# A graph attention, mixture-of-experts and graph convolution kernel: smaller expert groups with resident second weights, part rows gathered earlier, and a count's column table in PSUM

## The chip, the cores and the metric

One core of a Trainium2 chip runs the whole program. The metric is device microseconds (us) of one execution, as the median of the runs shown; the profile is of one further execution. The engines are TensorE (PE; its weight loads are listed apart as PEld), VectorE (DVE), ScalarE (ACT), GpSimd (POOL) and SyncE (SP, which only issues DMAs).

## What is computed

Four layers on 6250 nodes of 256 features and 200000 edges, each added to the residual `x` after a layer norm. Only the first two are touched by the change, and the third uses a table that the second prepares.

```python
# layer 1: graph attention, 8 heads of 32
e = leaky_relu(a_src[src] + a_dst[dst], 0.2)
e_exp = exp(e - segment_max(e, dst)[dst])
alpha = e_exp / (segment_sum(e_exp, dst)[dst] + 1e-16)
x = x + relu(segment_sum(h[src] * alpha[:, :, None], dst) + bias)
# layer 2: 8 experts, the best 2 for each node, 256 -> 512 -> 256
y = sum over e of (gelu(xn @ W1[e] + b1[e]) @ W2[e] + b2[e]) * w_full[..., e]
# layer 3: graph convolution with in and out degrees; layer 4: 8 experts with a capacity
```

## The kernel before

**The attention loop** (`gat_edges`, L1102) goes over 104 steps of 16 edge tiles. For each step POOL issues 16 gathers of 128 rows (L1262) into a ring of four buffers, and each engine works through a fixed order of parts of neighbouring steps, its `slot`. On DVE (L1432) a slot begins with `count_onehots` (L1337): two comparisons (L1344) of a column table `iob`, `count_iota` in SBUF in bfloat16, with the halves of the sources' numbers; TensorE later sums the one-hots to the degrees (L1525). After them come `totals` (L1349), which wait for the terms that TensorE turns (L1493) once the step's last gather has landed and ACT has packed its terms (L1274), then the sums into the residual (L1430) and the `messages` (L1407), which read the numerators that ACT wrote to PSUM (`numerators`, L1277). The end of a ring buffer's use, `sc`, lets POOL gather again (L1259).

**Rows and logits** (`rows_and_logits`, L1642, with `AttentionRows`, L1569) make the layer-1 result, its norm and the router's logits; SP meanwhile writes zeros over 12.8 MB of the expert output (`zero_fill`, L1772). **Routing** (`route`, L2430) is a chain on DVE that ends with 98 pairs of one-hot comparisons (L2593, L2594), each followed by a product on TensorE (L2631). POOL has nothing to do in it.

**The first experts** (`experts`, L2635) take the sorted slots in 56 groups of 256 (`TOK1`), each of one expert, in 14336 slots in all. For a group POOL gathers two tiles of rows (L2693), TensorE turns them (L2725), DVE scales them into `xT` (L2777), TensorE makes the hidden product from `w1s`, whose columns it takes with a stride of four (`f:F:FC`, L2735), ACT applies the activation (L2761), TensorE makes the output from `hT` and `w2s` (L2745), DVE adds `b2` (L2788), and POOL scatters two tiles (L2700). SP loads `w1`, `b1`, `w2` and `b2` of the group's expert for each group into one of two buffers (L2675 to L2679). A float32 product is two weight loads and two matmuls in the trace, a turn only one of each.

Beside the experts runs `DenseTables` (L708), which prepares the 62 code tables of layer 3: POOL gathers part rows (L755), DVE subtracts (L767), TensorE turns them in float32 (L782), ACT copies (L796), SP stores (L740). As there are only 56 groups, the last six run together in tick 1 (`rest`). `staged` (L142) orders the stages on every engine: two ticks written out for each of the first two rounds, then a loop of two ticks a round. On TensorE a tick is: hidden of the group before, turn of the codes, turn of this group, output of the group before.

The lines that order TensorE's tick and set the hidden product:

```python
staged(pe, groups, [(1, hidden), (1, side.turn(pe)), (0, turn), (1, outs)], 2)          # L2752
pe.matmul(ph[:, f % 2, 0:tok], w1s[:, b, c, f:F:FC], xT[:, b, c, :], start=c == 0, stop=c == 1)  # L2735
```

Of the kernel before, what the change touches and what calls it, by code (L numbers as in the profile page):

```python
# [19 lines left out]
P = 128  # L20
# [7 lines left out]
TOK1 = 256  # L28
# [91 lines left out]
class RoundTable:  # L120

    def __init__(self, nc, engine, row, depth, lag, top):
        self.nc, self.engine, self.row, self.depth, self.lag, self.top = nc, engine, row, depth, lag, top
        self.at = {}

    def fetch(self, i):
        start = i * self.depth - self.lag
        skip = -start if isinstance(start, int) and start < 0 else 0
        n = self.depth - skip
        _, values = self.nc.values_load_multi_w_load_instructions(
            self.row[:, bass.ds(start + skip, n)], engines=(self.engine,), min_val=0, max_val=self.top,
            skip_runtime_bounds_check_because="the table's rows were clamped to their range when they were built")
        for j in range(n):
            self.at[(skip + j - self.lag) % self.depth] = values[j]


def staged(eng, steps, stages, depth, tables=()):  # L142
# [15 lines left out]
    def fetch(i):  # L158
        for table in tables:
            table.fetch(i)  # L160

    rounds = steps // depth
    for i in range(2):
        fetch(i)
        for j in range(depth):
            tick(i, j)
    with eng.Fori(2, rounds) as i:
        fetch(i)
        for j in range(depth):
            tick(i, j)  # L170
    if any(lag for lag, _ in stages):
        fetch(rounds)
    for j in range(max(lag for lag, _ in stages)):
        tick(rounds, j)
# [532 lines left out]

class DenseTables:  # L708


    def __init__(self, k, S, C, T, ctx):
        self.nc, self.S, self.C, self.T = k.nc, S, C, T
        self.rest = S.SUPER - S.G1
        assert S.G1 % 2 == 0 and self.rest > 0
        self.rg = k.sems("part_rows_gathered", 2)
        self.xg = k.sem("rest_rows_gathered")
        self.xs = k.sem("rest_codes_stored")
# [4 lines left out]
        self.vr = k.sb(ctx, "part_rows", [P, 2, 2, P])  # L722
        self.vx = k.sb(ctx, "rest_rows", [P, self.rest, 2, P])
        self.row = k.sb(ctx, "codes_out", [P, 2, 2 * P], BF16)
        self.rx = k.sb(ctx, "rest_codes_out", [P, self.rest, 2 * P], BF16)
        self.pt = k.ps(ctx, "codes_ps", [P, 512])

    def order(self, t):

        return t if isinstance(t, int) and t < 2 else t + self.rest  # L730

    def rest_at(self, t):

        return range(self.rest) if isinstance(t, int) and t == 1 else ()

    def store(self, sp):
        def put(n, s, row, sem):
            sp.wait_ge(self.tc, n + 1)
            sp.nop(nofuse=True)
            sp.dma_start(self.T.codes[bass.ds(s, 1), :, :].rearrange("a p c -> p (a c)"), row).then_inc(sem, 16)  # L740

        def stage(i, b, t, first):
            put(self.order(t), t, self.row[:, b, :], self.cs[b])
            for x in self.rest_at(t):
                put(2 + x, self.S.G1 + x, self.rx[:, x, :], self.xs)
        return stage

    def stored(self, sp):
        for m in range(2):
            sp.wait_ge(self.cs[m], 16 * (self.S.G1 // 2))  # L750
        sp.wait_ge(self.xs, 16 * self.rest)

    def gather(self, pool, t):
        def take(s, out, sem):
            pool.indirect_dma_start(  # L755
                out=out.rearrange("p a e -> p (a e)"), out_offset=None, in_=self.T.gnn[:, :],
                in_offset=bass.IndirectOffsetOnAxis(ap=self.C.vpart[:, s:s + 1], axis=0)).then_inc(sem, 16)
        if t >= 2:
            pool.wait_ge(self.tp, self.order(t - 2) + 1)
        take(t, self.vr[:, t % 2, :, :], self.rg[t % 2])  # L760
        for x in self.rest_at(t):
            take(self.S.G1 + x, self.vx[:, x, :, :], self.xg)

    def compare(self, dve):
        def stage(i, b, t, first):
            dve.wait_ge(self.rg[b], i * 16 + 16)
            dve.tensor_scalar(self.vr[:, b, 0, :], self.vr[:, b, 0, :], self.C.vcode[:, bass.ds(t, 1)], None,  # L767
                              ALU.subtract).then_inc(self.cr, 1)
            for x in self.rest_at(t):
                s = self.S.G1 + x  # L770
                dve.wait_ge(self.xg, 16 * self.rest)
                dve.tensor_scalar(self.vx[:, x, 0, :], self.vx[:, x, 0, :], self.C.vcode[:, s:s + 1], None,
                                  ALU.subtract).then_inc(self.cr, 1)
        return stage

    def turn(self, pe):
        def turned(n, rows):
            pe.wait_ge(self.cr, n + 1)
            if not isinstance(n, int) or n >= 1:
                pe.wait_ge(self.tc, n)  # L780
            for a in range(2):
                last = pe.transpose(self.pt[:, a * P:(a + 1) * P], rows[:, a, :], self.C.ident[:, :])  # L782
            last.then_inc(self.tp, 1)

        def stage(i, b, t, first):
            turned(self.order(t), self.vr[:, b, :, :])
            for x in self.rest_at(t):
# [2142 lines left out]
```

## Time and profile before

| | us |
|---|---|
| three runs, median (lowest, highest) | 5123.05 (5122.59, 5126.46) |
| the profiled execution | 5124.75 |
| its span, first to last instruction | 5122.9 |
| PE, DVE, POOL, ACT busy in the span | 4174.7, 3459.0, 2300.1, 1648.5 |
| mean granted TensorE clock | 0.841 |

The span falls into stages that follow each other, with all engines meeting at the end of each. A busy share over the whole span says little, as the limit changes from stage to stage; a stage is read from its own stretch. The granted clock is a share of 2.4 GHz; it has two levels, 1.0 and 0.5, and a mean between them is a mixture.

### The profile page before, as it was taken

The page shows a single profiled execution, that of the slowest core. Times are in us where ns is not written, and L with a number is a line of the kernel's source. Part 1 is how long each engine was busy: PE and PEld are TensorE (multiplying, and loading weights), DVE is VectorE, ACT ScalarE, POOL GpSimd, SP SyncE. Part 2 cuts the span into 40 slices and gives each one's busy share as a digit, 9 for nine tenths or more (in the row PEclk, how much of TensorE's full clock was granted, in tenths as well). Part 3 has the DMA queues.
Part 4 walks back from the last instruction along what each step waited for, and adds up shares of the span by engine and source line. Part 5 has one row for each costly group of instructions (what it writes and reads, how often), then busy time and mean ns, then how long its engine had stood idle before and what let it go on. Part 6 is the DMA issues. An engine that isn't in the chain of part 4 may idle for free. (4 is left out here: it accounts for less than half of the span.)

```text
span 5122.9 us, 87171 instructions
## 1 busy us (share of the span) xinstructions
PE 4174.7 (81%) x27202; PEld 3066.2 (60%) x27203; DVE 3459.0 (68%) x7696; ACT 1648.5 (32%) x2854; POOL 2300.1 (45%) x2330
## 2 busy tenths in 40 slices
PE   3477777777777777776699964799999999958998
PEld 2355555555555555555489953466666666557787
DVE  6366766676667667768622237899998999764444
ACT  1233333333333333333122236333333333231211
POOL 1377777777777777774155620000000000024553
PEclk9677777777777777776799986899999999958999
DMA  4766666666666666656167653454545545453432
GB/s 122 188 164 164 168 162 164 163 169 162 163 165 168 162 163 165 167 157 207 63 218 232 233 176 111 87 98 85 97 87 90 93 89 95 85 184 115 136 122 87
DMA packets 978900, 733.38 MB, mean 143 GB/s; under 512 B 735781, under 2 KB 864352, under 8 KB 976628
## 3 DMA queue, kind: packets, MB, share of 16 engines
q1 hardware_dynamic: 863047, 427.75, 32.6%
q0 software_dynamic: 109264, 296.24, 21.0%
q10 hardware_dynamic: 6364, 6.40, 0.4%
q8 instruction: 141, 2.31, 0.2%
q14 instruction: 84, 0.68, 0.0%
HBM read 485.07 MB, written 92.30 MB: 113 GB/s over the span
## 5 line engine op out<-in xcount | busy, mean ns | idle before, releaser
L1262 POOL DMA_INDIRECT gat_rows<-h_rows,gat_sources x1664 | 1621.9, 975 | 509.9 <-issue 478.8
L1520 PE MATMUL gat_sum_ps<-gat_rows,gat_onehot 128*128 128x265 f32 x3328 | 1261.7, 542 | 3.7 <-DVE gat_rows L1407 3.6
L1520 PEld LDWEIGHTS gat_sum_ps<-gat_rows,gat_onehot 128*128 128x128 f32 x3328 | 861.3, 272 | 218.2 <-DVE gat_rows L1407 4.8
L2207 ACT CAST gnn_z<-build_ps 128x392 bf16<-128x392 f32 x992 | 479.7, 485 | 749.4 <-PE build_ps L2222 749.2
L2231 PE MATMUL back_ps<-zb_pieces,gnn_z 128*128 128x384 bf16 x3038 | 634.6, 325 | 0.0
L2253 PE MATMUL front_ps<-x_res_wide,front_rows 128*128 128x448 bf16 x2604 | 618.1, 351 | 0.0
L2148 DVE TENSOR_TENSOR onehot_low<-dense_codes,dense_iota_bf 128x2048 bf16<-128x2048 bf16 x496 | 603.9, 1218 | 2.0 <-PE build_ps L2222 1.9
L2127 POOL DMA_INDIRECT front_rows<-zf_piece_rows,vrow_nodes x62 | 58.8, 948 | 1148.0 <-PE front_ps L2253 1137.9
L1407 DVE TENSOR_TENSOR gat_rows<-gat_rows,gat_numerators_ps 128x1024 f32<-128x1024 f32 x416 | 502.2, 1207 | 0.0
L2222 PEld LDWEIGHTS build_ps<-onehot_high,onehot_low 128*128 128x128 bf16 x7936 | 352.6, 98 | 184.9 <-issue 38.2
L2735 PE MATMUL moe_hidden_ps<-moe_rows_T,moe_w 128*128 128x256 f32 (+1 forms) x1408 | 450.4, 475 | 2.3 <-DMA moe_b<-in_L_ffn_b 1.5
L2761 ACT ACTIVATE moe_hidden<-moe_hidden_ps,moe_b 128x256 f32<-128x256 f32 (+1 forms) x352 | 194.0, 551 | 765.3 <-PE moe_hidden_ps L2735 765.3
L2745 PE MATMUL moe_out_ps<-moe_w,moe_hidden 128*128 128x256 f32 x1920 | 434.8, 384 | 1.1 <-ACT moe_hidden L2761 1.1
L2735 PEld LDWEIGHTS moe_hidden_ps<-moe_rows_T,moe_w 128*128 128x128 f32 x1408 | 377.5, 322 | 65.3 <-issue 4.8
L2222 PE MATMUL build_ps<-onehot_high,onehot_low 128*128 128x49 bf16 x7936 | 373.5, 188 | 44.0 <-DVE onehot_high L2148 41.5
L1430 DVE TENSOR_TENSOR x_res_wide<-x_res_wide,gat_sum_ps 128x265 f32 x832 | 355.7, 428 | 66.9 <-DVE x_res_wide L1430 66.4
L2745 PEld LDWEIGHTS moe_out_ps<-moe_w,moe_hidden 128*128 128x128 f32 x1920 | 360.1, 190 | 63.0 <-issue 13.9
L2231 PEld LDWEIGHTS back_ps<-zb_pieces,gnn_z 128*128 128x128 bf16 x3038 | 263.2, 97 | 150.7 <-issue 1.3
L1280 ACT ACTIVATE gat_numerators_ps<-gat_exponents 128x128 f32<-128x128 f32 x104 | 29.3, 281 | 906.2 <-DVE gat_exponents L1400 759.4
L2160 DVE TENSOR_TENSOR gnn_z<-gnn_z,front_ps 128x448 f32<-128x448 f32 x434 | 267.8, 617 | 74.8 <-PE front_ps L2253 73.3
L1493 PE MATMUL gat_turned_ps<-ident,gat_src_terms 128*128 128x128 f32 x104 | 49.3, 474 | 324.7 <-ACT gat_src_terms L1274 324.7
L2253 PEld LDWEIGHTS front_ps<-x_res_wide,front_rows 128*128 128x128 bf16 x2604 | 222.9, 97 | 139.8 <-issue 0.3
(377 smaller groups left out, 5467.5 us busy)
## 6 DMA issues: line engine op xcount, KB each, us to landing
moe_w<-in_L_ffn_W SPq DMA_DIRECT2D x112, 512.0 KB
gat_targets<-gat_step_targets SPq DMA_DIRECT2D x104, 512.0 KB
moe_w<-in_L_ffn_w SPq DMA_DIRECT2D x32, 1024.0 KB
gat_rows<-h_rows,gat_sources POOLq DMA_INDIRECT x1664
gat_flags<-gat_tile_flags SPq DMA_DIRECT2D x104, 128.0 KB
normal_rows<-moe_xn_all SPq DMA_DIRECT2D x14, 896.0 KB
mid_taken<-moe_rows_out SPq DMA_DIRECT2D x14, 896.0 KB, 7.4
moe_rows_out<-slot_zeros SPq DMA_DIRECT2D x24, 512.0 KB
```

The source lines that it names most:

```text
L1262: pool.indirect_dma_start(out=g[:, b, t, :], out_offset=None, in_=T.h[:, :], in_offset=bass.IndirectOffsetOnAxis(ap=idx[:, b, t:t + 1], ax ...
L1407: dve.tensor_tensor(rows[:, :, :, 0:HD], rows[:, :, :, 0:HD], pW[:, n * PART:(n + 1) * PART, :].unsqueeze(3).to_broadcast([P, PART, H, HD] ...
L1430: dve.tensor_tensor(window(w), window(w), po[:, s % BANKS, 0:W], ALU.add).then_inc(ad, 1)
L1520: last = pe.matmul(po[:, s % BANKS, 0:W], o[:, b, s * SUB + t, :], g[:, b, s * SUB + t, :], start=t == 0, stop=t == SUB - 1)
L2148: last = dve.tensor_tensor(out[:, n, :, :, :], ct[:, k % SLOTS, a, at].rearrange("p (u t) -> p u t", t=HITS).unsqueeze(2) .to_broadcast(sh ...
L2160: dve.tensor_tensor(yfT[:, at:at + CN], yfT[:, at:at + CN], pf[:, n, 0:CN], ALU.add).then_inc(ya, 1)
L2207: nc.scalar.copy(AT[:, k % 2, :, CHUNK * c:CHUNK * (c + 1)], pb[:, c % 2, 0:CHUNK * NT].rearrange("p (u h) -> p h u", u=CHUNK)).then_inc(a ...
L2222: last = pe.matmul(pb[:, c % 2, u * NT:(u + 1) * NT], ol[:, n, i, :, t], oj[:, n, i, :, t], start=True, stop=True)
L2231: ins = pe.matmul(py[:, (k - 1) % 2, 0:3 * P], AT[:, (k - 1) % 2, h, :], zb3[:, h, :, :].rearrange("p s f -> p (s f)"), start=h == 0, stop ...
L2253: ins = pe.matmul(pf[:, bank, 0:CN], zfv[:, first + s, m * P:(m + 1) * P], AV[:, first + s, chunk * CN:(chunk + 1) * CN], start=n == 0, st ...
L2735: last = pe.matmul(ph[:, f % 2, 0:tok], w1s[:, b, c, f:F:FC], xT[:, b, c, :], start=c == 0, stop=c == 1)
L2745: last = pe.matmul(py[:, q % 2, 0:D], hT[:, f, q * P:(q + 1) * P], w2s[:, b, f, :], start=f == 0, stop=f == FC - 1)
```

## The change

- `TOK1` is 128: the first experts run in 106 groups of 128 slots (13568 slots), in a function of their own, `resident_experts`. The second weights of all eight experts (`w2`, 4 MB) and `b1` are loaded once by SP during rows and logits; `b2` of all experts once at the start of the experts. Per group SP loads only `w1`. The hidden product takes contiguous columns of `w1`. The output product and the biases take the expert by a register; each of PE, ACT and DVE loads four group numbers a round for that (`Choice.fetch`).
- The output of a group comes two ticks after its turn (one before), with two buffers for `hT` and a PSUM bank for each of the four hidden slices.
- All 62 gathers of part rows go to POOL in routing (`gather_parts`); the code tables are turned in bfloat16, in the first 62 ticks.
- Only the pad rows of the expert output are zeroed (2 DMAs of 22 rows instead of 25 DMAs).
- In the attention loop the column table of the count is a float32 table in PSUM, in the bank of the numerators; `count_onehots` waits for the numerators of its step first.

```diff
-TOK1 = 256
+TOK1 = 128
 class DenseTables:
+    def start(self, dve):
+        dve.tensor_copy(self.ident[:, :], self.C.ident[:, :]).then_inc(self.ir, 1)
+        dve.wait_ge(self.pg, 16 * self.S.SUPER)
     def compare(self, dve):
         def stage(i, b, t, first):
-            dve.wait_ge(self.rg[b], i * 16 + 16)
-            dve.tensor_scalar(self.vr[:, b, 0, :], self.vr[:, b, 0, :], self.C.vcode[:, bass.ds(t, 1)], None,
+            if not first:
+                dve.wait_ge(self.tp, t - 1)
+            rows = self.parts[:, bass.ds(t, 1), :, :].rearrange("p s a e -> p (s a) e")
+            dve.tensor_copy(self.code[:, b, 1, :], rows[:, 1, :])
+            dve.tensor_scalar(self.code[:, b, 0, :], rows[:, 0, :], self.C.vcode[:, bass.ds(t, 1)], None,
                               ALU.subtract).then_inc(self.cr, 1)
...
 gat_edges:
-        iob = k.sb(ctx, "count_iota", [P, P, 2], BF16)
-        pW = k.ps(ctx, "gat_numerators_ps", [P, TILES, H])
+        pWI = k.ps(ctx, "gat_numerators_ps", [P, 512])
+        pW = pWI[:, 0:TH].rearrange("p (t h) -> p t h", h=H)
+        iob = pWI[:, TH:TH + 2 * P].rearrange("p (w t) -> p w t", t=2)
             def count_onehots(j, i, a):
                 dve.wait_ge(cl[b], i * 16 + 16)
+                dve.wait_ge(ex, j + 1)
...
 AttentionRows.load:
-        self.filled = zero_fill(sp, [self.y1[0:2 * self.S.ROWS, :], *self.more], self.zf, self.zs)
+        pads = self.S.ROWS - self.S.N
+        for a in range(2):
+            sp.dma_start(self.y1[a * self.S.ROWS + self.S.N:(a + 1) * self.S.ROWS, :], self.zf[0:pads, :]).then_inc(self.zs, 16)
+        self.weights.load(sp)
...
 route:
+        if tables is not None:
+            @block.gpsimd
+            def _(pool):
+                gather_parts(pool, S, C, tables, k.parts, k.pg)
...
+def resident_experts(k, S, C, T, tag, groups, func, W, xn, y, src_of, dst_of, gtab, affine):
+        @block.sync
+            sp.dma_start(b2[:, :, :].rearrange("p e d -> p (e d)"), W.dram[3].rearrange("e d -> (e d)").partition_broadcast(P)).then_inc(bl, 16)
+            def load(i, b, t, first):
+                e = sp.value_load(gtab[0:1, bass.ds(t, 1)], min_val=0, max_val=W.X - 1)
+                if not first:
+                    sp.wait_ge(hp, (t - 1) * FC)
+                    sp.nop(nofuse=True)
+                sp.dma_start(w1s[:, b, :, :], W.dram[0][bass.ds(e, 1), :, :].rearrange("a (c p) f -> p (a c) f", p=P)).then_inc(wl[b], 16)
+            phased(sp, groups, [(0, None, load), (2, S.SUPER, side.store(sp))], 2)
+        @block.gpsimd
+            for t in range(groups + 4):
+                if t < groups:
+                    take(t)
+                if t >= 4:
+                    put(t - 4)
+        @block.tensor
+            def hidden(i, b, t, first):
+                pe.wait_ge(tc, t + 1)
+                pe.wait_ge(wl[b], i * 16 + 16)
+                for f in range(FC):
+                    if not (first and b == 0):
+                        pe.wait_ge(hc, t * FC + (f + 1 - FC))
+                    for c in range(2):
+                        last = pe.matmul(ph[:, f, 0:P], w1s[:, b, c, f * P:(f + 1) * P], xT[:, b, c, :],
+                                         start=c == 0, stop=c == 1)
+                    last.then_inc(hp, 1)
+            def outs(i, b, t, first):
+                e = expert.at(2, b)
+                pe.wait_ge(hc, t * FC + FC)
+                for f in range(FC):
+                    last = pe.matmul(py[:, b, 0:D], hT[:, b, f, :], W.w2[:, bass.ds(e, 1), f, :].rearrange("p a d -> p (a d)"),
+                                     start=f == 0, stop=f == FC - 1)
+            pe.wait_ge(side.ir, 1)
+            pe.wait_ge(W.wl, W.full)
+            phased(pe, groups, [(1, None, hidden), (1, S.SUPER, side.turn(pe)), (0, None, turn), (2, None, outs)], 2, expert.fetch)
+        @block.scalar
+            phased(act, groups, [(0, None, hidden), (0, S.SUPER, side.copy(act))], 2, expert.fetch)
+        @block.vector
+            dve.wait_ge(bl, 16)
+            side.start(dve)
+            phased(dve, groups, [(0, None, turned), (2, None, outs), (0, S.SUPER, side.compare(dve))], 2, expert.fetch)
```

`phased` is `staged` with a tick count at which a stage ends (62 for the code tables) and a call at the start of each round, in which the registers are loaded.

## Rows read from the trace of the kernel before

**Rows 1.** Busy by stretch: stretch, length, PE, PEld, DVE, ACT, POOL, clock, DMA, GB/s.
```profile
194.00:2324.00 2130.00, 1626.01 (x7892) 1170.55 (x7892) 1473.71 (x3799) 701.96 (x724) 1621.94 (x1664) 0.75 0.62 164
...
2454.00:2532.00 78.00, 46.55 (x200) 31.47 (x200) 70.73 (x275) 1.53 (x2) 0.00 (x0) 0.76 0.00 1
2543.00:3013.00 470.00, 465.46 (x2136) 422.00 (x2136) 120.00 (x284) 123.68 (x286) 270.55 (x279) 0.99 0.68 224
```

**Rows 2.** Groups, attention loop: count, busy us, mean ns, idle before by releaser.
```profile
L1262 POOL DMA_INDIRECT gat_rows<-h_rows,gat_sources x1664 | 1621.9, 975 | 509.9 <-issue 478.8 <-PE gat_sum_ps L1520 27.7 <-DMA gat_sources<-step_sources 3.4
...
L1407 DVE TENSOR_TENSOR gat_rows<-gat_rows,gat_numerators_ps 128x1024 f32<-128x1024 f32 x415 | 501.0, 1207 | 0.0
L1430 DVE TENSOR_TENSOR x_res_wide<-x_res_wide,gat_sum_ps 128x265 f32 x824 | 352.3, 428 | 65.8 <-DVE x_res_wide L1430 65.6 <-PE gat_sum_ps L1520 0.2
...
L1344 DVE TENSOR_TENSOR count_onehot_lo<-count_halves,count_iota 128x2048 bf16<-128x2048 bf16 x104 | 127.4, 1225 | 63.9 <-PE gat_sum_ps L1520 62.2 <-issue 1.8
...
L1344 DVE TENSOR_TENSOR count_onehot_hi<-count_halves,count_iota 128x784 bf16<-128x784 bf16 x104 | 58.2, 559 | 0.0
```

**Rows 3.** Timeline of one attention step: start us, length us, engine, line, idle before.
```profile
1202.17 1.22 DVE L1407 TENSOR_TENSOR gat_rows<-gat_rows,gat_numerators_ps 128x1024 f32<-128x1024 f32 x1
1202.55 0.94 POOL L1262 DMA_INDIRECT gat_rows<-h_rows,gat_sources  x1 [0.30 <-issue]
...
1214.53 0.21 ACT L1283 ACTIVATE gat_factors<-gat_exponents 1x8 f32<-1x8 f32 x1
...
1215.12 0.95 POOL L1262 DMA_INDIRECT gat_rows<-h_rows,gat_sources  x1 [0.30 <-issue]
1215.58 1.23 DVE L1344 TENSOR_TENSOR count_onehot_lo<-count_halves,count_iota 128x2048 bf16<-128x2048 bf16 x1 [0.51 <-PE gat_sum_ps L1520]
...
1216.37 1.25 POOL L1262 DMA_INDIRECT gat_rows<-h_rows,gat_sources  x1 [0.30 <-issue]
...
1220.51 0.42 DVE L1353 TENSOR_TENSOR_SCAN gat_running<-gat_flags,gat_turned_ps 128x128 f32<-128x128 f32 x1 [3.23 <-PE gat_turned_ps L1493]
```

**Rows 4.** Timeline of TensorE in one tick of the first experts.
```profile
2701.11 4.07 PE L2735 MATMUL moe_hidden_ps<-moe_rows_T,moe_w 128*128 128x256 f32 x16
2705.01 0.38 PE L782 MATMUL codes_ps<-ident,part_rows 128*128 128x128 f32 x2
2705.23 0.60 PE L2725 MATMUL moe_turn_ps<-ident,moe_rows 128*128 128x128 f32 x4
2705.81 3.71 PE L2745 MATMUL moe_out_ps<-moe_w,moe_hidden 128*128 128x256 f32 x16
2709.37 0.93 PE L2735 MATMUL moe_hidden_ps<-moe_rows_T,moe_w 128*128 128x256 f32 x3
```

**Rows 5.** Timeline of the weight loads in a stretch of the attention loop.
```profile
1206.61 0.52 PEld L1504 LDWEIGHTS gat_small_ps<-gat_tile_carries,gat_head_select_T 8*128 8x128 f32 x4 [0.35 <-issue]
1207.05 0.08 PEld L1506 LDWEIGHTS gat_small_ps<-ident,gat_previous 8*1 8x1 f32 x1
```

**Rows 6.** Timeline at the start of the first experts.
```profile
2542.94 5.76 PE L2735 MATMUL moe_hidden_ps<-moe_rows_T,moe_w 128*128 128x256 f32 x16 [1.02 <-DMA moe_b<-in_L_ffn_b]
...
2569.25 2.97 PE L2735 MATMUL moe_hidden_ps<-moe_rows_T,moe_w 128*128 128x256 f32 x12
```

**Rows 7.** Timeline at the end of the first experts.
```profile
3009.07 3.72 PE L2745 MATMUL moe_out_ps<-moe_w,moe_hidden 128*128 128x256 f32 x16 [0.34 <-ACT moe_hidden L2761]
```

**Rows 8.** DMA issues by line, whole span: KB each, median us from issue to landing.
```profile
unit_codes<-codes_out SPq DMA_DIRECT2D x56, 64.0 KB, 4.8
```

**Rows 9.** Timeline around the start of routing: last logits copy, first operation.
```profile
2453.68 0.17 ACT L1738 COPY moe_raw_logits<-moe_po 128x8 f32<-128x8 f32 x1 [1.06 <-PE moe_po L1768]
...
2454.16 0.57 DVE L2498 TENSOR_TENSOR moe_logits<-moe_raw_logits,b_router 128x392 f32<-128x392 f32 x1 [17.00 <-PEq L1658]
```

**Rows 10.** Timeline at routing's end.
```profile
2531.43 0.22 DVE L2606 TENSOR_SCALAR moe_slot_source<-moe_slot_token 128x112 int32<-128x112 f32 x1
```

**Rows 11.** Timeline of SP's DMA issues in rows and logits.
```profile
2370.65 25.17 SPq L1779 DMA_DIRECT2D moe_rows_out<-slot_zeros  x25
```

More of the change, by code:

```diff
@@ L117, in join, with staged @@
         self.eng.wait_ge(self.sem, self.n)
[L120 to L142, printed above, removed]
+def staged(eng, steps, stages, depth):
     def tick(i, j):
@@ L749, in stored @@
         for m in range(2):
[L750 to L762, printed above, removed]
+            sp.wait_ge(self.cs[m], 16 * (self.S.SUPER // 2))
@@ L781, in turned @@
             for a in range(2):
-                last = pe.transpose(self.pt[:, a * P:(a + 1) * P], rows[:, a, :], self.C.ident[:, :])
+                last = pe.transpose(self.pt[:, a * P:(a + 1) * P], self.code[:, b, a, :], self.ident[:, :])
             last.then_inc(self.tp, 1)
-        def stage(i, b, t, first):
-            turned(self.order(t), self.vr[:, b, :, :])
-            for x in self.rest_at(t):
-                turned(2 + x, self.vx[:, x, :, :])
         return stage
@@ L2661, in experts @@
         py = k.ps(ctx, f"{tag}_out_ps", [P, 2, 512])
-        side = DenseTables(k, S, C, tables, ctx) if tables is not None else None
         if final is not None:
@@ L2705, in _ @@
                     take(t)
-                if side is not None and 1 <= t <= groups:
-                    side.gather(pool, t - 1)
                 if t >= 2 and final is None:
@@ L2747, in outs @@
                     last.then_inc(yp, 1)
[L2749 to L2752 removed]
+            staged(pe, groups, [(1, hidden), (0, turn), (1, outs)], 2)
         @block.scalar
@@ new lines, with __init__, fetch, at @@
+class Choice:
+    def __init__(self, nc, engine, table, top):
+        self.nc, self.engine, self.table, self.top = nc, engine, table, top
+    def fetch(self, i):
+        first = max(2 * i - 2, 0) if isinstance(i, int) else i * 2 - 2
+        n = min(2 * i + 2, self.table.shape[1]) - first if isinstance(i, int) else 4
+        _, self.values = self.nc.values_load_multi_w_load_instructions(
+            self.table[0:1, bass.ds(first, n)], engines=(self.engine,), min_val=0, max_val=self.top,
+            skip_runtime_bounds_check_because="the groups' experts were clamped to their range when they were written")
+        self.shift = 2 - (2 * i - first) if isinstance(i, int) else 0
+    def at(self, lag, slot):
+        back = -(-(lag - slot) // 2) if lag > slot else 0
+        return self.values[2 - 2 * back + slot - self.shift]
```

244 lines of the change are left out of this document (170 added, 74 removed).

## The prediction

> **What bounds the kernel now.** I read the clock and busy time by stretch first, because the limit changes from stage to stage, and then three stages that the change touches [rows 1]. In the attention loop (2130 us) no engine is near full by its busy share: PE 1626, POOL 1622, DVE 1474. The groups by line give the answer: POOL's 1664 gathers are busy 1621.9 us and idle 509.9 us before themselves, and of that 478.8 is "issue", its own 0.30 us between two gathers [rows 2]. Busy and issue fill the stretch, so POOL bounds this loop, at 0.95 + 0.30 = 1.25 us a gather, 16 gathers a step. One step's timeline shows what makes it longer: the gather at 1216.37 takes 1.25 where its neighbour takes 0.95, and it is the one that starts while DVE compares for the count (L1344); DVE itself then waits 3.23 us for the terms TensorE turns, which wait for the gathers' landing [rows 3]. In the first experts (470 us) PE is busy 465 at a granted clock of 0.99, DVE 120, ACT 124, POOL 271: TensorE bounds it [rows 1]. Routing (78 us) is DVE's, busy 71, with POOL idle [rows 1].
>
> **The attention loop.** Mean gather 975 ns, unhindered 0.95 us: 1664 x 0.025 = 41 us of lengthening [rows 2, 3]. Both comparisons read two tables in SBUF; the sums (L1430) and messages (L1407) read one in SBUF and one in PSUM, run all through the loop, and the gather beside a message keeps 0.94 [rows 3]. With its table in PSUM the count becomes of that second kind, so I take the whole 41 us off. The price is on DVE: L1430 and L1407 take 428 ns for 265 columns and 1207 for 1024, that is 156 ns and 1.03 ns a column, so 2048 and 784 columns take 2.26 and 0.96 us in place of 1.23 and 0.56 [rows 2]: 1.43 us more a step. It lies before `totals`, where DVE waits 3.23 us; with a step 0.4 us shorter about 1.4 us of that wait is left, so it is covered. If the cover were gone, each uncovered 0.1 us a step would cost 10 us. The new wait for the numerators holds up the whole DVE slot, but ACT's last numerator write starts at 1214.53 and ends 0.8 us before the count begins [rows 3]: nothing. Only in the last slots, with no gather behind them, one longer count shows: 1.4 us. Sum: **-40 us**. Bounds: 0 if the lengthening has another cause, -57 with every gather at 0.94.
>
> **The first experts.** A tick of 256 slots runs from hidden to hidden 8.26 us: hidden 16 records from 2701.11 to 2705.01, 0.244 each; two code turns 0.22; four turns to the output's start 0.58; output 16 records to 2709.37, 0.2225 each [rows 4]. In the new tick of 128 slots the output has 8 records of the same form, 1.78. The hidden product has 16 records of 128 columns and not 256. Its nearest rows are the turns: pairs of a contiguous 128-column weight load and a 128-column matmul start every 0.11 us (2705.01 to 2705.23) [rows 4]. That this also holds for weights of an ordinary float32 product is seen in the attention loop, where four such loads follow each other in 0.44 us, 0.11 each [rows 5]. The 0.244 today against 0.2225 for the output is the strided load, which goes. So 16 x 0.11 = 1.76, and two turns 0.22. The codes' turns in bfloat16 have no row; between nothing and 0.22 for two I take 0.11, in 62 of 106 ticks. The 0.14 us that now lies between turns and output is a wait for the activation; an output that lags two ticks has its input long before. I leave 0.05 a tick for register loads. A tick: 1.76 + 0.22 + 1.78 + 0.06 + 0.05 = 3.87 us, 106 of them 410 us. The last output adds 2, the first ticks at the lower clock 4 (the first hidden product takes 5.76 for 4.07 [rows 4, 6]): 416 us. Today the same stretch is from 2542.94 to 3009.07 + 3.72, 470 us [rows 6, 7]; that includes some 10 us for the six `rest` codes and the slow first ticks, as 2569.25 is the third hidden product and two ticks take 16.5. Sum: **-54 us**.
>
> What must stay hidden: one `w1` load. Today w1, b1, w2 and b2 (1.16 MB) leave just before the code store on one queue, and that store, last of them, lands 4.8 us after its issue, with no wait for weights on PE; at the stretch's 224 GB/s 512 KB take 2.3 us [rows 1, 8], so one `w1` lands between 2.3 and 4.8 us after its issue, an estimate. It is issued when the hidden product two groups back ends and needed two ticks after that one began: 7.7 - 1.8 = 5.9 us. POOL issues 212 gathers and scatters at 0.97 + 0.30, 270 us of 410; DVE and ACT stay under half. Bounds of the tick: 3.72 with no gaps; 5.7 if a 128-column record cost as much as a 256-column one, which the 0.11 speaks against.
>
> **Routing and what moves.** POOL gets 62 gathers at 1.25 us, 77.5 us. Routing runs from 2454.16 to 2531.65, 77.5 us [rows 9, 10] and a little longer with 106 groups in its tables. The two chains are even, so each lengthened gather counts. In routing's first 30 us most DVE operations read two SBUF tables; 24 gathers fall there, and at 0.30 a hit, with all or none hit, that is 0 to 7 us. I take the queue of POOL to end 5 us after DVE's old end: **+5 us**. The zeros (25 DMAs, 25.17 us of SP's issuing [rows 11]) give way to 2 pad and 9 weight DMAs; the stage ends with ACT's logits copy at 2453.68 [rows 9], so nothing. `b2` (1 MB) now precedes the first `w1` on SP and holds back DVE, and with it the first turn; today 1.16 MB lies before the first hidden product: nothing, bounds -2 and +4.
>
> **Sum.** 5124.75 - 40 - 54 + 5 = 5036 for the profiled execution, which is 1.7 us over the median; so 5034 us. About 0.2% (10 us) is what a measurement of this kernel can tell from no change.
>
> **Rivals.**
> *The gathers stay long.* What lengthens them is DVE's load on SBUF as such, or the next operation takes the count's place under a gather. For it: only one place of a step shows it. Against: L1430 and L1407 write as much. Time: 5034 + 41 = 5075. Chance 0.10.
>
> *Weight loads set the pace of the hidden product.* With 128 columns a load is no longer shorter than its matmul, and a little that does not overlap shows in each of 1696 records. At 0.16 a record, about the middle between the 0.11 of 128 columns and the 0.2225 of 256, the tick is 0.80 longer: 106 x 0.80 = 85, 5119 us. Against: pairs at 0.11 [rows 4, 5], though those are few in a row. The Trainium skill, "TensorE: Matmul & The Clock Gate", section "Back-to-back issue gap", says a stream of load and matmul pairs at 128 columns sustains about 81 ns where an isolated gap would be 56; by that ratio the 0.11 would be the 0.16 of this rival. The trace disagrees as far as its short runs go. Chance 0.08, half of it faster and half the same.
>
> *Slower: TensorE's clock falls.* Twice as many hand-overs (turn, copy by DVE, hidden product) in each 256 slots; if one is late in each tick, by the weights or the turned rows, PE is no longer full. The attention loop, with PE busy 1626 of 2130, is granted a mean of 0.75, the experts 0.99 [rows 1]. At the lower level a tick doubles to 7.6 us and the stage to some 810 us: 5430. It decides from a tick of 4.7 us: 106 x 4.7 + 6 = 504, which eats 470 plus the 35 gained elsewhere. Against: two copies of 128 columns take DVE 0.6 us by the same 156 ns and 1.03 ns a column, and the 1.78 us of output lie between. Chance 0.07, with DVE's longer count overrunning its 1.4 us of cover on the same side.
>
> *Routing holds on longer*, POOL 15 us behind: 5044, chance 0.08, inside the range.
>
> **How the numbers follow.** The forecast has 0.67, with 5013 (tick without gaps, routing even) to 5060 (tick 4.1). The range 5010 to 5080 adds the first and last rivals, 0.85 together. Faster: 0.67 + 0.10 + 0.08 + 0.04 = 0.89; same 0.04; slower 0.07.
>
> **What would show it.** In the profile after: L1262's mean at 0.95 and the loop near 2090 us; L1344 at 2.3 and 1.0 us; DVE's wait before L1353 near 1.4; hidden records every 0.11 us and hidden to hidden 3.9 us at a clock of 1.0; POOL's gathers filling routing. I am wrong if L1262 still shows 1.25 us gathers once a step, if PE waits for weights or turned rows in the experts, or if their clock is under 0.95.

## The result and the profile after

The changed kernel takes **5030.49 us** (median of four runs, 5029.82 to 5031.65) where the kernel before takes 5124.76 beside it (5122.59 to 5126.56): a ratio of 0.9817, 95% interval 0.9805 to 0.9829. The forecast was 5034 us, faster. The profiled execution has a span of 5028.0 us, 94.9 less than the 5122.9 before.

Where the 94.9 us come from is read off the two timelines at the same landmarks. Up to the first gather 2.1 us are lost, which is spread: in the traces of the runs below with the same code there, the first gather starts between 194.0 and 198.3 us. From the first gather to the out-degrees, the attention loop with its tail, it is 2161.8 against 2119.9 us: -41.9, of which the gathers give -44.6 and the tail behind the last gather, with one longer count in the way, takes back 2.7 (33.4 to 36.1; 33.3 again in the run below with the table back in SBUF). From there to the first operation of routing: nothing (97.3 both times). From that to the first hidden product 88.8 against 92.6: +3.8. From the first hidden product to the end of the last output 469.9 against 410.5: -59.3. The rest of the program: +0.4.

Busy time by stretch comes first (stretch, length, PE, PEld, DVE, ACT, POOL, clock, DMA, GB/s): attention loop, routing with the wait behind it, first experts, as in [rows 1].

```profile
197.00:2281.00 2084.00, 1573.86 (x7892) 1116.37 (x7892) 1623.56 (x3798) 701.88 (x724) 1577.22 (x1664) 0.78 0.63 168
2414.30:2500.50 86.20, 45.85 (x200) 32.17 (x200) 72.51 (x275) 1.53 (x2) 61.27 (x62) 0.74 0.30 95
2507.00:2925.00 418.00, 408.78 (x2878) 380.65 (x2878) 142.02 (x440) 173.21 (x487) 203.65 (x210) 0.99 0.64 207
```

POOL lost 45 us of busy time in the first line and DVE gained 150, POOL now works in the second, and the third is shorter at the same clock of 0.99. The groups of the attention loop answer to [rows 2] (count, busy us, mean ns, idle before by releaser):

```profile
L1244 POOL DMA_INDIRECT gat_rows<-h_rows,gat_sources x1664 | 1577.2, 948 | 510.0 <-issue 486.5 <-PE gat_sum_ps L1503 20.1 <-DMA gat_sources<-step_sources 3.4
...
L1327 DVE TENSOR_TENSOR count_onehot_lo<-count_halves,gat_numerators_ps 128x2048 bf16<-128x2048 bf16 x103 | 235.6, 2288 | 68.0 <-PE gat_sum_ps L1503 45.8 <-issue 21.4 <-ACT gat_factors L1265 0.8
...
L1327 DVE TENSOR_TENSOR count_onehot_hi<-count_halves,gat_numerators_ps 128x784 bf16<-128x784 bf16 x103 | 99.3, 964 | 0.0
...
L1336 DVE TENSOR_TENSOR_SCAN gat_running<-gat_flags,gat_turned_ps 128x128 f32<-128x128 f32 x103 | 43.3, 421 | 202.5 <-PE gat_turned_ps L1476 202.5
```

The mean gather went from 975 to 948 ns with the same 510 us of idle time between gathers, so all of the loop's gain is in the gathers' own length. The comparisons went from 1.23 and 0.56 us to 2.29 and 0.96, and DVE's wait for the turned terms (L1336, L1353 before) from 350.9 / 103 = 3.41 us a step to 202.5 / 103 = 1.97. The line of the kernel before:

```profile
L1353 DVE TENSOR_TENSOR_SCAN gat_running<-gat_flags,gat_turned_ps 128x128 f32<-128x128 f32 x103 | 43.3, 421 | 350.9 <-PE gat_turned_ps L1493 350.9
```

One step's timeline (start us, length us, engine, line, idle before) shows the place:

```profile
1196.13 0.20 ACT L1265 ACTIVATE gat_factors<-gat_exponents 1x8 f32<-1x8 f32 x1
...
1197.24 2.29 DVE L1327 TENSOR_TENSOR count_onehot_lo<-count_halves,gat_numerators_ps 128x2048 bf16<-128x2048 bf16 x1 [0.58 <-PE gat_sum_ps L1503]
...
1198.30 0.95 POOL L1244 DMA_INDIRECT gat_rows<-h_rows,gat_sources  x1 [0.30 <-issue]
...
1199.45 0.96 DVE L1327 TENSOR_TENSOR count_onehot_hi<-count_halves,gat_numerators_ps 128x784 bf16<-128x784 bf16 x1
...
1199.55 0.95 POOL L1244 DMA_INDIRECT gat_rows<-h_rows,gat_sources  x1 [0.30 <-issue]
...
1202.15 0.42 DVE L1336 TENSOR_TENSOR_SCAN gat_running<-gat_flags,gat_turned_ps 128x128 f32<-128x128 f32 x1 [1.74 <-PE gat_turned_ps L1476]
```

Both gathers under the comparisons keep 0.95 us. ACT's last operation of the numerators (1196.13) is over before the count begins; over all steps the new wait holds 0.8 us ("ACT gat_factors" in the group above). TensorE's tick in the first experts answers to [rows 4]:

```profile
2700.57 1.95 PE L2892 MATMUL moe_hidden_ps<-moe_rows_T,moe_w 128*128 128x128 f32 x16
2702.36 0.28 PE L771 MATMUL codes_ps<-codes_ident,part_codes 128*128 128x128 bf16 x2
2702.47 0.39 PE L2882 MATMUL moe_turn_ps<-ident,moe_rows 128*128 128x128 f32 x2
2702.69 1.89 PE L2902 MATMUL moe_out_ps<-moe_w,moe_hidden 128*128 x8
2704.42 1.95 PE L2892 MATMUL moe_hidden_ps<-moe_rows_T,moe_w 128*128 128x128 f32 x16
```

3.85 us from hidden to hidden for 128 slots, with 16 hidden records in 1.79 us, 0.112 each; in the 44 ticks without codes it is 3.73 (2852.38 to 2856.11). Not every tick is so even. Of the 62 ticks with codes 14, every fourth, take 4.06 to 4.09 us, and the tick behind each takes 3.95:

```profile
2610.07 1.95 PE L2892 MATMUL moe_hidden_ps<-moe_rows_T,moe_w 128*128 128x128 f32 x16
...
2614.14 2.05 PE L2892 MATMUL moe_hidden_ps<-moe_rows_T,moe_w 128*128 128x128 f32 x16
```

Every second tick TensorE loads group numbers into its registers (`Choice.fetch`). In these 14 ticks that load lasts some 1.27 us, and the next weight load starts 0.3 us after its end; in the ticks between them it lasts 0.34 to 0.59. So it reads as the register load that holds these ticks back, 4.6 us in all; no run takes it out. Before, 256 slots took 8.26 us in the tick of [rows 4], but 8.17 in the median of all ticks:

```profile
2799.86 3.98 PE L2735 MATMUL moe_hidden_ps<-moe_rows_T,moe_w 128*128 128x256 f32 x16
...
2808.03 3.98 PE L2735 MATMUL moe_hidden_ps<-moe_rows_T,moe_w 128*128 128x256 f32 x16
```

The one surprise is the end of routing [rows 10]:

```profile
2493.21 0.40 DVE L2593 TENSOR_SCALAR moe_slot_source<-moe_slot_token 128x106 int32<-128x106 f32 x1
...
2493.88 0.95 POOL L718 DMA_INDIRECT unit_part_rows<-gnn_part_rows,vrow_part  x1 [0.31 <-issue]
...
2500.19 0.35 SPq L2840 DMA_DIRECT2D moe_b<-in_L_ffn_b  x1
...
2500.83 0.94 POOL L2856 DMA_INDIRECT moe_rows<-normal_rows,moe_slot_source  x1 [6.00 <-POOLq L2437]
```

DVE ends at 2493.61 and POOL's last part gather at 2494.83, and then nothing is issued on any queue for 5.4 us. The first take comes 7.22 us after DVE's end, 6.00 after that gather's. Before, it came 1.15 us after DVE's end.

### The profile page after: what moved, and what is told of

It is laid out like the page before. It is cut to its first block and busy times, and to the rows that moved or that the text cites. A ratio compares the mean times of both kernels' runs of the same rounds, so it can differ in the third digit from the quotient of the medians.

```text
span 5028.0 us, 91035 instructions
## 1 busy us (share of the span) xinstructions
PE 4063.6 (81%) x27942; PEld 2970.5 (59%) x27943; DVE 3635.7 (72%) x7853; ACT 1698.4 (34%) x3055; POOL 2243.8 (45%) x2318
## 5 line engine op out<-in xcount | busy, mean ns | idle before, releaser
L1244 POOL DMA_INDIRECT gat_rows<-h_rows,gat_sources x1664 | 1577.2, 948 | 510.0 <-issue 486.5
L1503 PE MATMUL gat_sum_ps<-gat_rows,gat_onehot 128*128 128x265 f32 x3328 | 1169.7, 510 | 7.2 <-DVE gat_rows L1390 6.4
L1503 PEld LDWEIGHTS gat_sum_ps<-gat_rows,gat_onehot 128*128 128x128 f32 x3328 | 792.6, 250 | 196.9 <-DVE gat_rows L1390 5.8
L1327 DVE TENSOR_TENSOR count_onehot_lo<-count_halves,gat_numerators_ps 128x2048 bf16<-128x2048 bf16 x104 | 237.9, 2288 | 68.3 <-PE gat_sum_ps L1503 45.8
L2135 DVE TENSOR_TENSOR onehot_high<-dense_codes,dense_iota_bf 128x784 bf16<-128x784 bf16 x496 | 277.0, 558 | 0.0
L2920 ACT ACTIVATE moe_hidden<-moe_hidden_ps,moe_b 128x128 f32<-128x128 f32 x424 | 155.7, 368 | 233.0 <-PE moe_hidden_ps L2892 211.8
L2743 ACT ACTIVATE moe_hidden<-moe_hidden_ps,moe_b 128x512 f32<-128x512 f32 x128 | 88.0, 688 | 417.8 <-PE moe_hidden_ps L2720 417.8
L2720 PE MATMUL moe_hidden_ps<-moe_rows_T,moe_w 128*128 128x512 f32 x512 | 225.7, 599 | 0.8 <-DVE moe_rows_T L2754 0.8
```

Source lines behind the costliest of these rows:

```text
L1244: pool.indirect_dma_start(out=g[:, b, t, :], out_offset=None, in_=T.h[:, :], in_offset=bass.IndirectOffsetOnAxis(ap=idx[:, b, t:t + 1], ax ...
L1327: last = dve.tensor_tensor(out[:, :, :, :], hl[:, b, half, :].rearrange("p (u t) -> p u t", t=2).unsqueeze(2).to_broadcast(shape), iob[:, ...
L1503: last = pe.matmul(po[:, s % BANKS, 0:W], o[:, b, s * SUB + t, :], g[:, b, s * SUB + t, :], start=t == 0, stop=t == SUB - 1)
L2135: last = dve.tensor_tensor(out[:, n, :, :, :], ct[:, k % SLOTS, a, at].rearrange("p (u t) -> p u t", t=HITS).unsqueeze(2) .to_broadcast(sh ...
L2720: last = pe.matmul(ph[:, f % 2, 0:tok], w1s[:, b, c, f:F:FC], xT[:, b, c, :], start=c == 0, stop=c == 1)
```

## The experiments

Twelve runs; each time below is a median, and differences to the changed kernel are taken from its 5030.49 us unless another is named.

### Why the gathers got shorter

**Table back in SBUF**, the rest as changed:

```diff
-        iob = pWI[:, TH:TH + 2 * P].rearrange("p (w t) -> p w t", t=2)
+        iob = k.sb(ctx, "count_iota", [P, P, 2], BF16)
...
-                dve.wait_ge(ex, j + 1)
```

> The changed kernel with the count's column table back in SBUF in bfloat16, all else as changed. Theory (the comparison of two SBUF operands lengthens one or two of the 16 gathers of a step): gathers of over 1.1 us come back, the mean gather goes from 948 to about 975 ns, the comparison falls from 2.29 to 1.23 us, and the time rises by what the attention loop had gained, 38 to 46 us, to 5068 to 5077 us. Rival (the loop's gain came from something else of the change): 5025 to 5036 us, no gather above 1.1 us.

**Table in SBUF in float32**: the same edit without `BF16`.

> The column table in SBUF but in float32, so that the comparison reads two SBUF operands and is still about as long as from PSUM (2.3 us and 0.96 us a step). Theory A (two SBUF operands lengthen the gathers): gathers of over 1.1 us come back, at least as much as with bfloat16, since the comparison lasts 1.8 times as long: 5068 to 5115 us. Theory B (only the short comparison, with both operands of two bytes, lengthens them): gathers stay at 0.95 us, 5025 to 5036 us.

Measured: 5075.41 us with bfloat16, 5166.25 with float32. The groups of the loop, first bfloat16:

```profile
L1244 POOL DMA_INDIRECT gat_rows<-h_rows,gat_sources x1664 | 1622.7, 975 | 509.9 <-issue 481.6 <-PE gat_sum_ps L1502 25.0 <-DMA gat_sources<-step_sources 3.4
...
L1326 DVE TENSOR_TENSOR count_onehot_lo<-count_halves,count_iota 128x2048 bf16<-128x2048 bf16 x104 | 127.5, 1226 | 64.0 <-PE gat_sum_ps L1502 58.5 <-issue 5.5
```

with a step of it,

```profile
1219.13 1.22 DVE L1326 TENSOR_TENSOR count_onehot_lo<-count_halves,count_iota 128x2048 bf16<-128x2048 bf16 x1 [0.51 <-PE gat_sum_ps L1502]
...
1219.92 1.25 POOL L1244 DMA_INDIRECT gat_rows<-h_rows,gat_sources  x1 [0.30 <-issue]
```

then float32:

```profile
L1244 POOL DMA_INDIRECT gat_rows<-h_rows,gat_sources x1664 | 1714.7, 1030 | 510.0 <-issue 479.2 <-PE gat_sum_ps L1502 27.4 <-DMA gat_sources<-step_sources 3.4
...
L1326 DVE TENSOR_TENSOR count_onehot_lo<-count_halves,count_iota 128x2048 bf16<-128x2048 bf16 x103 | 236.6, 2297 | 63.8 <-PE gat_sum_ps L1502 52.8 <-issue 11.0
```

The undone part gives back 44.9 us (42.7 of them between the first gather and the out-degrees), all of what the loop had gained, and the old 975 ns. The float32 table is the clean proof: that comparison lasts as long as the one from PSUM (2297 against 2288 ns), differs from it in where its second operand lies, and costs 135.8 us. So it is not the comparison's length, nor two-byte operands, but the second operand in SBUF. The size was beyond the 5115 us that theory A had allowed. A step of the float32 run shows why:

```profile
1218.05 2.31 DVE L1326 TENSOR_TENSOR count_onehot_lo<-count_halves,count_iota 128x2048 bf16<-128x2048 bf16 x1 [0.99 <-PE gat_sum_ps L1502]
...
1219.28 1.89 POOL L1244 DMA_INDIRECT gat_rows<-h_rows,gat_sources  x1 [0.30 <-issue]
...
1220.28 0.96 DVE L1326 TENSOR_TENSOR count_onehot_hi<-count_halves,count_iota 128x784 bf16<-128x784 bf16 x1
...
1221.47 0.94 POOL L1244 DMA_INDIRECT gat_rows<-h_rows,gat_sources  x1 [0.30 <-issue]
```

The gather that starts at 1219.28, under the comparison, ends at 1221.17, 0.81 us after the long comparison's record (1220.36); in the step with bfloat16 it is 0.82 us (1221.17 after 1220.35). Taken over all steps the two traces, and that of the kernel before, say the same: 82 gathers before, 84 with bfloat16 and 103 with float32 start under the long comparison and are lengthened beyond 1.1 us, and all but one of these 269 end 0.81 to 0.83 us after it, while the second comparison ends 0.34 us before the gather with bfloat16 and 0.07 us after it with float32 (medians). So the gather is held until the long comparison lets go, and the second does not hold it on. A gather that already runs when the comparison starts is not lengthened (0.94 to 0.96 us in all three traces).

That gives the sizes. With bfloat16 84 of 104 steps have such a gather, 1.46 us long in the mean, 0.51 lost: 43 us; with float32 103, 2.25 us long, 1.31 lost: 135 us. The runs have 44.9 and 135.8. A comparison 1.9 times as long costs three times as much: more steps are hit, and what is left of the comparison when a gather starts is longer, while a gather loses that rest less some 0.13 us (0.95 less 0.82).

The Trainium skill, "SBUF — State Buffer", section "Who interferes with whom", states that a VectorE instruction with two SBUF inputs contends with a GpSimd instruction that reads SBUF, that one with at most one SBUF input, outside the modes that use both ports, does not, and that the shared ports are an exclusive lock. The rows above agree: held until the end, not slowed in part, and 0.95 us beside the PSUM table. The section's remark that a `tensor_tensor` was not seen to stall a DMA of GpSimd does not hold for these gathers, which read their row numbers (`gat_sources`) from SBUF: here the measurement decides.

### What the order of the weights is worth

**Strided at 128 columns**: the changed kernel with the old order of hidden units (`b1` and `w2` laid out to match).

```diff
-                        last = pe.matmul(ph[:, f, 0:P], w1s[:, b, c, f * P:(f + 1) * P], xT[:, b, c, :],
+                        last = pe.matmul(ph[:, f, 0:P], w1s[:, b, c, f:F:FC], xT[:, b, c, :],
```

> The changed kernel with the first experts' weights again taken every fourth column (hidden unit 4p+f in partition p; first bias and second weights laid out to match). Theory A (the 128 columns set the pace of a product, the weights' order hardly): a record of the hidden product goes from 0.112 us to at most 0.12, 8 to 14 us in 106 ticks of 16, 5030 to 5045 us. Theory B (reading strided weights sets the pace, as long for 128 columns as for 256): a record of about 0.23 us, a tick longer by 1.9 us, 5200 to 5235 us. Something between tells how long a strided load takes.

**In a row at 256 columns**: the kernel before with `f * P:(f + 1) * P` in the first experts' hidden product, `b1` and `w2` left as they were; it serves for its time alone.

> The kernel before, groups of 256 slots, with the first experts' weights taken in a row in the hidden product and nothing else changed (the first bias and second weights stay where they were, so they meet other hidden units than the reference wants). Theory A (a strided load of 0.23 us is longer than 256 columns take, so it sets the pace there too): a record goes from 0.24 to about 0.2225 us, 56 ticks of 16 records, 9 to 19 us less than before, 5106 to 5117 us. Theory B (at 256 columns the matmul hides the load): 5122 to 5129 us, as before.

Measured: 5223.89 us, 193 more than the changed kernel, theory B almost to its full size; and 5110.45 beside 5127.0 for the kernel before, a ratio of 0.9969 (0.9958 to 0.9981), 16 us less, theory A. Ticks of the strided run:

```profile
2799.47 3.79 PE L2892 MATMUL moe_hidden_ps<-moe_rows_T,moe_w 128*128 128x128 f32 x16
...
2803.43 1.89 PE L2902 MATMUL moe_out_ps<-moe_w,moe_hidden 128*128 x8
2805.16 3.79 PE L2892 MATMUL moe_hidden_ps<-moe_rows_T,moe_w 128*128 128x128 f32 x16
```

and of the kernel before with its weights in a row:

```profile
2700.07 3.67 PE L2735 MATMUL moe_hidden_ps<-moe_rows_T,moe_w 128*128 128x256 f32 x16
...
2707.93 3.66 PE L2735 MATMUL moe_hidden_ps<-moe_rows_T,moe_w 128*128 128x256 f32 x16
```

The weight loads of the hidden product, first in the changed kernel, then in the strided run:

```profile
L2892 PEld LDWEIGHTS moe_hidden_ps<-moe_rows_T,moe_w 128*128 128x128 f32 x1696 | 206.3, 193 | 13.5 <-issue 6.4 <-DVE moe_rows_T L2934 2.4
```

```profile
L2892 PEld LDWEIGHTS moe_hidden_ps<-moe_rows_T,moe_w 128*128 128x128 f32 x1664 | 396.2, 328 | 2.7
```

Sixteen strided records take 3.62 us to the next matmul (2803.09), 0.226 each for 128 columns, where 256 columns in a row take 0.219 (to 2703.57) and 128 in a row 0.112. The clock is 0.99 in all of them, and a weight load's own record goes from 193 to 328 ns. A strided float32 weight load thus sets a pace of about twice its matmul's at 128 columns. At 256 columns it was already the longer of the two, but only a little: 0.238 us a record in the median of the kernel before (0.244 in the tick of [rows 4]) against 0.219, and a tick of 7.86 us in place of the median 8.17.

With it the experts' 59.3 us can be split: 15.5 are the row order at 256 columns (first hidden product to the degrees' root 481.2 against 465.6 us). Then 56 ticks of 7.86 are 440.2 us and 62 of 3.85 with 44 of 3.73 are 402.8, which makes 37.4. Of these 6 x 3.93 = 23.6 are the six groups of 128 slots that smaller groups save (106 for 112), and the other 13.8 are the shorter tick: for 256 slots 7.70 us with codes and 7.46 without, for 7.86. By the rows this is the wait of 0.14 us ahead of the output, which is gone, and ticks that no longer have codes; the later output and the bfloat16 turns were not undone one by one. The remaining 6 are the difference of what lies outside the even ticks: some 14 us in the kernel with its weights in a row, most of it in the first three ticks with the six `rest` codes; in the changed kernel 1.4 in the first ticks, 4.6 in the 14 longer ones and 1.7 for the last output, which comes a tick later.

### The 6 us behind routing

**40 part gathers in routing, 22 in the experts' loop**, one a tick after `take`, with one wait for these on VectorE:

```diff
-    for s in range(S.SUPER):
+    for s in range(40):
...
+                if 2 <= t < S.SUPER - 40 + 2:
+                    gather_part(pool, C, T, k.parts, side.pl, 40 + t - 2)
...
+            if isinstance(t, int) and t == 40:
+                dve.wait_ge(self.pl, 16 * (self.S.SUPER - 40))
```

> The changed kernel with 40 of the 62 part gathers in routing and 22 in the first experts' loop on GpSimd, one a tick beside take and put, and one wait for these on VectorE at tick 40. Theory A (the 6.00 us between routing and the first take is GpSimd's last gathers, for whose landing the end of the block waits): the gap falls to about 1.1 us, routing's VectorE time may fall by up to 1.7 us, 5022 to 5026 us. Theory B (the gap belongs to the new experts' start, whatever GpSimd did before): the gap stays at 6 us, 5029 to 5033 us.

**48 and 14**, with the changed kernel once more on the same chip:

> As the run with 40 part gathers in routing, with 48 there and 14 in the experts' loop. If the end of routing waits for GpSimd's last gathers, 48 are early enough too (48 x 1.29 = 62 us of routing's 79): gap 1.1 us, 4 to 8 us less than the changed kernel run beside it. If 40 was only a faster draw of the attention loop's gathers: no difference to it.

> The changed kernel itself, for comparison on one chip with the run with 48 part gathers in routing: 5029 to 5032 us.

Measured: 5024.28 us with 40; 5021.93 with 48 (5018.17 to 5025.77) beside 5032.52 for the changed kernel (5029.31 to 5035.05). The end of routing with 48:

```profile
2489.29 0.22 DVE L2602 TENSOR_SCALAR moe_slot_source<-moe_slot_token 128x106 int32<-128x106 f32 x1
...
2490.01 0.35 SPq L2849 DMA_DIRECT2D moe_b<-in_L_ffn_b  x1
...
2490.65 0.94 POOL L2865 DMA_INDIRECT moe_rows<-normal_rows,moe_slot_source  x1 [17.89 <-POOLq L2446]
```

The first take comes 1.14 us after VectorE's end again, with 40 too, so the 6 us belong to gathers issued shortly before the stage's end: theory A by the gap. The trace tells a part of what passes in them: in the changed kernel the last gather's rows land at 2496.95, 2.1 us after its end, and the first issue comes 3.2 us after that landing; why these 3.2 us pass stays open. From routing's first operation to the degrees' root it is 507.9 us with 40, 508.8 with 48 and 515.4 in the changed kernel run beside the 48: 6.6 to 7.5 us, which is the gap and a little of the experts. The rest of the 10.6 us between the medians is not the edit's: with 48 the stages ahead of routing ended 4.3 us earlier in the profile, with 40 they ended 4.9 us later, and the code is the same. Routing itself stays at 79.0 us of VectorE with 40 or 48 gathers, 79.3 with all 62, so the last gathers cost it 0.3. Of the 1.8 us over the old 77.5, two operations over 848 columns of the groups' tables in place of 448 make 0.83 (0.63 and 0.62 us became 1.04 each). Beside the gathers some short operations of unchanged shape are longer too, with 48 as with 62 (one of 128x49 takes 0.44 for 0.19 us), so POOL's part is more than the 0.3. These two kernels are the fastest of the study; against the kernel before 48 gives 0.9799 (0.9786 to 0.9813), the changed kernel 0.9819 (0.9805 to 0.9832).

### How much cover the longer count has left

A sum over PSUM columns that nothing uses is put ahead of the two comparisons (here over 8 x 256 columns; then 4, 2 and 6 x 256):

```diff
+                dve.tensor_reduce(spare[:, :], pWI[:, TH:TH + 2 * P].unsqueeze(1).to_broadcast([P, 8, 2 * P]), AX.X, ALU.add)
                 for out, half, w in ((ohl, 1, P), (ohh, 0, NT)):
```

> The changed kernel with one more VectorE operation ahead of each step's two comparisons, a sum over 2048 columns read from PSUM that nothing uses, about 2.2 us a step. Theory A (the cover is the 1.97 us that VectorE waits at the count's end, and VectorE bounds the step beyond it): 104 x 0.2 to 0.4 = 20 to 40 us more, 5050 to 5071 us. Theory B (VectorE's other waits of the step, 0.4 us and more, give way too): 5027 to 5036 us. Theory C (no cover; each microsecond shows): 5240 us and more.

> As the run with the added sum, over 1024 columns (about 1.15 us a step). The whole of 2.2 us cost 173 us, 1.67 a step, though VectorE's wait at that place is 1.97. Theory A (0.54 us of the wait can be used, and beyond it VectorE's chain through TensorE bounds the step one for one): 104 x 0.6 = 63 us more, 5085 to 5100 us. Theory B (the 1.97 us can be used, and beyond it a second loss sets in): 5028 to 5036 us. Theory C (nothing of it can be used, each added microsecond costs 0.76): 5110 to 5130 us.

> The same over 512 columns (about 0.58 us a step). Theory A (0.54 us can be used): 5030 to 5042 us. Theory B (1.97 us can be used): 5028 to 5034 us. Theory C (each added microsecond costs 0.76): 46 us more, 5070 to 5082 us.

> The same over 1536 columns. Over 512 and 1024 columns it took 0.69 and 1.22 us and cost at most 4 us in all, and VectorE's wait for the turned terms fell from 1.86 us a step to 1.27 and 0.79; over 2048 columns it took 2.29 us, the wait was gone, and 173 us were lost. Theory B (the wait can be used to its end, and the loss sets in where it is gone): 1.75 us, some 0.3 us of wait left, 5029 to 5038 us. Theory D (the loss sets in earlier, with VectorE's later terms in TensorE's way): 5060 us or more with some of the wait left.

Measured: 512 columns (0.69 us a step) 5034.07 us and 1024 (1.22 us) 5032.44, beside the changed kernel's 5032.52 on that chip; 2048 (2.29 us) 5203.95. With 1536 columns (1.76 us) the four runs fall into two groups: 5036.6 once, and 5137.3 to 5141.6 three times; the profiled one is of the three. What remains of VectorE's wait, from the groups of 512, 1024 and 1536 columns, one line of each kernel:

```profile
L1338 DVE TENSOR_TENSOR_SCAN gat_running<-gat_flags,gat_turned_ps 128x128 f32<-128x128 f32 x102 | 42.9, 420 | 129.6 <-PE gat_turned_ps L1478 129.6
```

```profile
L1338 DVE TENSOR_TENSOR_SCAN gat_running<-gat_flags,gat_turned_ps 128x128 f32<-128x128 f32 x102 | 42.9, 420 | 80.6 <-PE gat_turned_ps L1478 80.1
```

```profile
L1338 DVE TENSOR_TENSOR_SCAN gat_running<-gat_flags,gat_turned_ps 128x128 f32<-128x128 f32 x97 | 40.1, 413 | 6.1 <-PE gat_turned_ps L1478 6.1
```

and, with 2048, that line beside the two waits that came in its place:

```profile
L1338 DVE TENSOR_TENSOR_SCAN gat_running<-gat_flags,gat_turned_ps 128x128 f32<-128x128 f32 x94 | 38.9, 414 | 5.0 <-PE gat_turned_ps L1478 5.0
...
L1362 DVE CUSTOM_DVE_ANT_0 gat_junk<-gat_small_ps,gat_tile_select 128x16 f32<-128x16 f32 x188 | 25.4, 173 | 204.6 <-PE gat_small_ps L1491 203.9 <-issue 0.8
...
L1482 PE MATMUL gat_small_ps<-gat_tile_totals,gat_head_select 128*8 128x32 f32 x188 | 22.4, 204 | 234.8 <-DVE gat_tile_totals L1342 233.5 <-ACT gat_onehot L1282 1.3
```

With 512 and 1024 columns, where 1.27 and 0.79 us of wait a step are left, the added work costs nothing: theory B there, and the first guess of 0.54 us of usable cover was wrong. Past the wait's end the price is not what sticks out: with 2.29 us all four runs lost 171 to 183, where 0.3 to 0.4 us a step would have been some 40. In that run TensorE stands idle for VectorE's totals, 2.5 us a step (1.3 us in all 102 steps of the same stretch of the changed kernel), and VectorE then waits 2.2 us for TensorE's carries (204.6 us in all, 86.6 in the changed kernel). So two engines that each take their work in a fixed order wait for one another in turn. The trace shows the change from one rhythm to the other: in the third to eighth step TensorE's wait for the totals is 0.0, from the ninth on it is 1.4 to 3.5 us, and VectorE's steps then take 21.8 us in the mean for the 20.0 of the changed kernel, with the same gathers of 0.947 us.

The run with 1536 columns stands at the edge: 1.76 us is a little less than the changed kernel's wait of 1.86 (189.9 us in 102 steps). The profiled execution, one of the three long ones, has the long rhythm from its third step to the end of the loop (21.1 us a step), and its experts and all that follows take as long as in the changed kernel (412.1 and 2111.7 us for 410.5 and 2110.5). What made one execution of 5036.6 us and three long ones is open, and theories B and D are not told apart there.

### The zero fill

The changed kernel with `zero_fill` over all slot rows again.

> The changed kernel with the old zero fill of all slot rows in place of the pad rows alone: 25 more DMAs on SyncE in the rows and logits stage, ahead of the nine weight loads. Theory (they lie beside the stage's other work): 5027 to 5034 us, as the changed kernel. Rival (SyncE's 25 us of issuing hold back the experts' weights, which TensorE and ScalarE wait for): up to 25 us more, 5040 to 5056 us.

Measured: 5030.85 us (5029.85 to 5032.26) against 5030.49. The 25 DMAs lie beside the stage's other work.

## Why the prediction was right

The sum came out 3.5 us from the measured time. Its change, -89 us, is 5 short of the measured -94.3, and the kernel before took 1.7 us more beside the changed one than the median from which the sum started. Term by term:

- **Attention loop**, -40 predicted, -41.9 measured to the out-degrees. The step that mattered, one SBUF operand in place of two, holds: the table alone, moved back, costs 44.9 us. The rival with long gathers is what the bfloat16 table gives: 5075 predicted, 5075.41 measured. The comparisons took 2.29 and 0.96 us for 2.26 and 0.96, by the 1.03 ns a column. The wait left is 1.97 us where 1.4 was worked out: before it was 3.41 us in the mean (350.9 in 103 steps) and not the 3.23 of the step shown, and the shorter step took nothing from it. The last slots lost 2.7 us and not 1.4. One sentence failed: "each uncovered 0.1 us a step would cost 10 us". With 0.3 to 0.4 us a step past the edge it was 173 in all, and not some 40.
- **First experts**, -54 predicted, -59.3 measured. The even tick is 3.85 us with codes, as 3.87 had it, with 0.11 for two bfloat16 turns as taken, and 3.73 without, close to the bound of 3.72 (whose own terms add up to 3.76). 44 ticks at 0.14 less are 6 us. The 0.05 a tick for register loads is near in size, 4.6 us for 5.3, but it comes as 0.33 in each of 14 pairs of ticks. "The 0.244 today against 0.2225 for the output is the strided load, which goes": shown, 16 us, from a record of 0.238 in the median tick. The prediction did not see that at 128 columns the same load would have cost 193 us; the row order is no extra there but what makes the change pay: without it the change as a whole is a loss, 5223.89 us against 5126.14 for the kernel before on that chip.
- **The weight-load rival** (0.16 us a record): 16 records in a row take 0.112 each, and the rival is out for weights in a row. The ratio of 81 to 56 ns of the Trainium skill, "TensorE: Matmul & The Clock Gate", section "Back-to-back issue gap", from which the same 0.16 follows as an estimate, thus does not carry over to these float32 products. **The clock** stayed at 0.99, since the turned copies, 0.41 us each where I had 0.29, still end under the output's 1.73.
- **Routing**, +5 predicted, +3.8 measured, but not by the step I gave. POOL's queue ended 1.2 us after VectorE, not 5; 61.27 us busy for 62 gathers is 0.99 each, little lengthened. Instead the first take came 7.22 us after VectorE's end and not 1.15, and 4.01 came back because it is followed by the hidden product in 6.12 us and not 10.14. VectorE's 1.77, the 6.07 and the -4.01 make the 3.8. The sum is right by luck, its terms are wrong: the end of a stage for a queue that has just issued gathers was missing from it.
- **Zeros** at nothing: shown. **b2 ahead of the first weights**, -2 to +4: it lies inside those 6.12 us and was not tried by itself.

## What to carry to other kernels

When GpSimd issues gathers back to back, look for VectorE operations that read both inputs from SBUF: one input in PSUM nearly doubled the operation's time here and still won 45 us. With fewer columns on TensorE a strided weight load is no longer hidden, so the weights' layout comes first. And a wait that covers new work can be used, but not to its end: with 0.79 us a step left nothing was lost here, and past the end the loss was some four times what stuck out.

## What the runs showed of the hardware that was not expected

- A strided float32 weight load (every fourth column) sets a pace of 0.226 us a record, against 0.112 for 128 columns in a row.
- A gather that starts under a VectorE comparison with both inputs in SBUF ends 0.81 to 0.83 us after that comparison, in 268 of 269 cases; one that already runs keeps its 0.95 us. In the mean a gather so met takes 1.46 us under a comparison of 1.23 and 2.25 under one of 2.30.
- After a stage whose last act on POOL is a gather, nothing is issued for 5.4 us, 3.2 of them after its rows have landed; with the last gather some 17 us before VectorE's end the next stage starts 1.1 us after that end.
- In the ticks with codes a load of four group numbers into TensorE's registers takes 0.34 to 0.59 us or some 1.27, by turns; a tick with the long one is 0.2 us longer.
- One execution can go from one rhythm of a loop to another, 20.0 to 21.8 us a step, once its cover is used up, and stay there.
